# Experts of a routed block: the second product with the activations stationary, five tiles of 128 slots, and the last rows from GpSimd

## The chip, the core and the metric

The kernel runs on one core of one Trainium2 chip. Its time is the device time of one execution in microseconds (us). A core has TensorE (PE, with its weight loads listed apart as PEld), VectorE (DVE), ScalarE (ACT), GpSimd (POOL) and SyncE (SP), which issues most DMAs. Each engine takes its own instructions in order, and they meet through semaphores.

## What is computed

4096 tokens (32 sequences of 128) are embedded, pass one causal attention layer, and then a feed-forward layer with eight experts. Each token goes to one expert, and an expert takes at most 641 tokens. All arithmetic is float32. The part that matters here:

```python
capacity = int(N / E * CAPACITY_FACTOR) + 1          # 4096 / 8 * 1.25 + 1 = 641
eb = buf[:E * capacity].reshape(E, capacity, D)      # D = 256
h = gelu(einsum('ecd,edf->ecf', eb, W1) + b1[:, None, :])   # F = 1024
y = einsum('ecf,efd->ecd', h, W2) + b2[:, None, :]
out = where(valid, y[slot], 0.0) * combine_w[:, None]       # added to the residual
```

## The kernel before

The first part (up to 322 us of the profile) is attention and routing. It writes one row of 260 floats for each routed token to a DRAM table `rows_of_slots`: the residual (256), the routing weight (column D), mean and reciprocal deviation of the layer norm (D+1, D+2) and the token's number (D+3). Each expert has SL = 648 rows there.

The second part, `expert_phase`, does the experts one after the other, all on one core. 641 slots are rounded up to six tiles of 108 (NT = 6, TS = 108, SL = 648), or two halves of 324 columns (NH). float32 products are made of rounded pairs: a value x is kept as a high part (`hh`, `weh`, `xh`, written by ACT as a rounded copy) and a low part (`hl`, `wel`, `xl`, the difference, made by DVE), and each product takes three matmuls, high by high, high by low, low by high. For one expert the engines do this:

- **Up product** (L1260, 16 steps u): the weights are stationary (128 x 128), the tokens move (324 columns). A step is 6 matmuls into one of four PSUM banks S0, S1, C0, C1. ACT makes the gelu `gl` (L1184) and its rounded copy `hh` (L1178), and DVE makes `hl` (L1342). In the last six steps DVE also normalises the next expert's tokens (`xne`, L1304).
- **Down product** (L1277, 4 steps v): W2 is stationary, `hh`/`hl` move (324 columns), 24 matmuls a step, into banks PV and M2 in turn. The result stands with the features on the partitions. ACT adds the bias b2 (`yt`, L1199), PE transposes it back (`back`, L1227, 12 transposes of 128 x 108 into C0 and C1 for an expert, tiles 0 to 2 within the down product and 3 to 5 after steps u = 0 and u = 1 of the next expert), DVE multiplies by the routing weight and adds the residual (`finish`, `ys`, L1329), and POOL scatters the rows of a tile to the output by an indirect DMA (L1138).
- **For the next expert**, within the down product: ACT rounds W1 and W2 in eight pieces of 512 columns (`weh`, L1152), DVE subtracts (`wel<-w_raw,weh`, L1294, both inputs in SBUF, two pieces in each step v), PE transposes the normalised tokens (`turn`, L1215, three times four transposes), ACT and DVE make `xh` and `xl` of them.
- **SP** loads the weights of the expert after next into `w_raw`, then waits for all six scatters of the present expert and loads the next rows (L1104).

The bank of step v is free for step v + 2 when `yt` has been made.

Of the kernel before, what the change touches and what calls it, by code (L numbers as in the profile page):

```python
# [75 lines left out]
def lm_block(nc, x, table, wq, wk, wv, wo, wg, W1, b1, W2, b2, out):  # L76
# [28 lines left out]
    with ExitStack() as whole:  # L105
# [68 lines left out]
def attention_phase(nc, sb_in, sem, v):  # L174
    x, table, wq, wk, wv, wo, wg, b1, b2 = (v[n] for n in ("x", "table", "wq", "wk", "wv", "wo", "wg", "b1", "b2"))
# [15 lines left out]
    with ExitStack() as scope:  # L191
# [25 lines left out]
        bias_raw = sb("bias_raw", [E * (FC + KC), P], F32)  # L217
# [108 lines left out]
        def sync(sp):  # L326
# [4 lines left out]
            sp.dma_start(bias_raw[0:E * FC, :], b1.rearrange("e (c p) -> (e c) p", p=P)).then_inc(d_c, 16)  # L331
            sp.dma_start(bias_raw[E * FC:, :], b2.rearrange("e (c p) -> (e c) p", p=P)).then_inc(d_c, 16)
# [21 lines left out]
            def step(n, i):  # L354
# [270 lines left out]
        def tensor(pe):  # L625
# [30 lines left out]
            pe.wait_ge(d_c, 48)  # L656
            pe.transpose(bC[0][:, 0:E * (FC + KC)], bias_raw[:, :], identf[0:E * (FC + KC), 0:E * (FC + KC)]
# [184 lines left out]
        def vector(dve):  # L842
# [70 lines left out]
            dve.tensor_copy(biases[:, :], bC[0][:, 0:E * (FC + KC)]).then_inc(v_bias, 1)  # L913
# [140 lines left out]
def expert_phase(nc, sb_in, sem, v):  # L1054
    D, E, KC, F, FC, SL, NT, TS, NH, N = (v[n] for n in ("D", "E", "KC", "F", "FC", "SL", "NT", "TS", "NH", "N"))
# [5 lines left out]
    down_bank = [bPV, bM2]  # L1061
    turn_bank = [bM0, bM1]
    back_bank = [bC[0], bC[1]]
    NU = 2 * FC
    DOWN = 2 * KC
    TURNS = NT // 2
    PIECES = 8
    PC = 2 * KC * F // PIECES
    assert KC * F == FC * D and TURNS % 2 == 1

    with ExitStack() as scope:
# [3 lines left out]
        xs = [sb(f"xs{q}", [TS, NT, ROW], F32) for q in range(2)]  # L1075
        xn = sb("xne", [TS, NT, D], F32)
# [10 lines left out]
        d_out = [sem(f"d_out{j}") for j in range(NT)]  # L1087
        e_turn, e_up, e_down, e_back = sem("e_turn"), sem("e_up"), sem("e_down"), sem("e_back")
        a_xh, a_weh, a_gelu, a_hh, a_yt = (sem("a_" + n) for n in ("xh", "weh", "gelu", "hh", "yt"))
        v_exn, v_xl, v_wel, v_hl, v_ys = (sem("v_" + n) for n in ("exn", "xl", "wel", "hl", "ys"))  # L1090
# [10 lines left out]
        def sync(sp):  # L1101

            def load_rows(e):
                sp.dma_start(xs[e.slot][:, :, :], slots[bass.ds(e.times(SL), SL), :].rearrange("(p j) c -> p j c", j=NT)  # L1104
                             ).then_inc(d_xs[e.slot], 16)

# [3 lines left out]
            rows_of = slots[0:SL, :].rearrange("(p j) c -> p j c", j=NT)  # L1110
            for r in range(TURNS):
                sp.dma_start(xs[0][:, 2 * r:2 * r + 2, :], rows_of[:, 2 * r:2 * r + 2, :]).then_inc(d_first[r], 16)
            load_rows(expert(0, 1))

            def step(n, i):
                e, e2 = expert(n, i), expert(n, i + 2)
                if e2:
# [6 lines left out]
                    for j in range(NT):  # L1124
                        hold(sp, d_out[j], e.times(16, 16))
# [3 lines left out]
            for j in range(NT):  # L1129
                sp.wait_ge(d_out[j], 16 * E)  # L1130
# [255 lines left out]
```

## Time and profile before

| | |
|---|---|
| median of 3 runs | 595.01 us (592.73 to 596.51) |
| the profiled execution | 592.0 us, its span 590.3 us |
| granted TensorE clock over the span | 0.969 |
| PE busy | 543.5 us (92%) |
| one expert (from one down product to the next, mean of seven) | 31.05 us |
| from the last expert's down product to the end of the span | 29.3 us |

The profiled execution is 3.0 us below the median of the runs. The profile's page gives busy times of the engines, the chain of work that ended last, and groups of instructions by line. The trace behind it lists single instructions with start and duration.

### The profile page before, as it was taken

Reading aid. Unit: us, or ns where it says so; the run is one execution under the profiler, and the core shown is the slowest. Engines: PE = TensorE matmul, PEld = TensorE weight load, DVE = VectorE, ACT = ScalarE, POOL = GpSimd, SP = SyncE. Lnnn points to the kernel's source line nnn. Section 1 sums busy time; section 2 is a strip of 40 time slices with the busy share of each in tenths; the row PEclk is TensorE's granted clock in tenths of the full one; section 3 lists DMA queues with packets and bytes.
Section 4 is the critical chain, followed back from the end, with each engine's and each line's share of the span. In section 5 each row is a group of like instructions: output and inputs, shape, how many; then the busy total and the mean of one; then the engine's idle time right before and its main releaser. Section 6 shows DMA issues by size and latency. Waiting matters only on the chain.

```text
span 590.3 us, 13904 instructions
## 1 busy us (share of the span) xinstructions
PE 543.5 (92%) x5040; PEld 472.2 (80%) x5045; DVE 398.7 (68%) x1076; ACT 349.2 (59%) x760; POOL 264.8 (45%) x345
## 2 busy tenths in 40 slices
PE   6857899999999999998887999999999999999991
PEld 3646687787788887775553899999999999999990
DVE  7346689999999999988545475656575655665511
ACT  3323666666666666664523676858594949494820
POOL 6745677768667766765534004040403122121212
PEclk9977999999999999998899899999999999999996
DMA  3799986777777777771113601515150606020000
GB/s 111 190 269 274 280 258 215 239 248 235 235 224 218 234 234 229 200 234 61 38 47 108 190 1 39 191 40 191 31 195 22 202 13 197 28 72 8 29 6 27
DMA packets 44611, 86.51 MB, mean 147 GB/s; under 512 B 7614, under 2 KB 33779, under 8 KB 40896
## 3 DMA queue, kind: packets, MB, share of 16 engines
q1 hardware_dynamic: 37632, 72.83, 40.0%
q0 software_dynamic: 6144, 12.67, 6.9%
q8 instruction: 41, 0.67, 0.5%
q10 hardware_dynamic: 768, 0.13, 0.1%
q14 instruction: 26, 0.21, 0.1%
HBM read 52.64 MB, written 31.74 MB: 143 GB/s over the span
## 4 chain that ended last, share of the span: by engine, by line
PE 76%; DVE 8%; POOL 4%; issue 4%; DMA 4%; ACT 1%; SPq 1%; POOLq 0%; ACTq 0%; DVEq 0%
PE M L689 13%; PE M L1277 10%; PE PV L1277 10%; PE S L1260 10%; PE C L1260 10%; PE PV L835 6%; PE S L728 5%; PE C L741 4%; PE M L631 3%; PE M L710 2%; PE C L1227 2%; DVE mx L921 2%; PE M L1215 2%; DMA ks<-k_parts 1%; POOL h L431 1%
## 5 line engine op out<-in xcount | busy, mean ns | idle before, releaser
L1138 POOL DMA_INDIRECT out_dram<-ys,xs x48 | 51.1, 1064 | 212.4 <-DVE ys L1329 202.6
L536 ACT ACTIVATE pt<-C 128x512 f32<-128x512 f32 x128 | 76.4, 597 | 65.9 <-PE C L741 65.3
L483 POOL TENSOR_SCALAR_AFFINE_SELECT pt<-pt 128x512 f32<-128x512 f32 x128 | 81.1, 640 | 46.1 <-ACT pt L536 45.2
L921 DVE TENSOR_REDUCE mx<-S 128x4 f32<-128x512 f32 x128 | 86.7, 681 | 6.6 <-PE S L728 6.3
L1342 DVE TENSOR_TENSOR hl<-gl,hh 128x324 fp32r<-128x324 f32 x128 | 63.3, 495 | 37.7 <-ACT hh L1178 37.2
L728 PE MATMUL S<-ks,qs 128*128 128x128 bf16 x512 | 52.2, 227 | 10.9 <-issue 6.0
L1178 ACT ACTIVATE hh<-gl 128x324 fp32r<-128x324 f32 x128 | 59.2, 469 | 0.0
L728 PEld LDWEIGHTS S<-ks,qs 128*128 128x128 bf16 x512 | 30.2, 100 | 35.7 <-issue 26.0
L835 PE MATMUL PV<-pt,va 128*32 128x128 f32 x1024 | 55.3, 289 | 3.3 <-ACT os L546 1.6
L741 PE MATMUL C<-qs,ks 97*128 97x128 bf16 x512 | 51.5, 224 | 0.6 <-DMA qs<-nm 0.6
L1329 DVE SCALAR_TENSOR_TENSOR ys<-C,xs 108x256 f32<-108x256 f32 x48 | 21.7, 480 | 40.2 <-PE C L1227 40.2
L1294 DVE TENSOR_TENSOR wel<-w_raw,weh 128x512 fp32r<-128x512 f32 x64 | 40.8, 683 | 0.7 <-ACT weh L1152 0.7
L1260 PE MATMUL S<-xh,weh 128*128 128x324 f32 x128 | 41.2, 322 | 0.0
L1277 PE MATMUL M<-hh,weh 128*128 128x324 f32 x128 | 41.1, 321 | 0.0
L1277 PE MATMUL PV<-hh,weh 128*128 128x324 f32 x128 | 40.4, 316 | 0.0
L1260 PE MATMUL C<-xh,weh 128*128 128x324 f32 x128 | 40.3, 315 | 0.0
L1260 PE MATMUL S<-xl,weh 128*128 128x324 f32 x128 | 39.9, 312 | 0.0
L1277 PE MATMUL M<-hh,wel 128*128 128x324 f32 x128 | 39.9, 312 | 0.0
L1184 ACT ACTIVATE gl<-S,biases 128x324 f32<-128x324 f32 x64 | 34.1, 535 | 9.7 <-PE S L1260 9.7
L1277 PE MATMUL M<-hl,weh 128*128 128x324 f32 x128 | 39.9, 311 | 0.0
L1277 PE MATMUL PV<-hl,weh 128*128 128x324 f32 x128 | 39.9, 311 | 0.0
L1277 PE MATMUL PV<-hh,wel 128*128 128x324 f32 x128 | 39.9, 311 | 0.0
(170 smaller groups left out, 1608.8 us busy)
## 6 DMA issues: line engine op xcount, KB each, us to landing
w_raw<-in_L_ffn_W_dram SPq DMA_DIRECT2D x32, 512.0 KB, 7.5
qs<-q_parts SPq DMA_DIRECT2D x48, 256.0 KB, 4.4
ks<-k_parts SPq DMA_DIRECT2D x48, 256.0 KB, 6.0
q_parts<-qp SPq DMA_DIRECT2D x16, 384.0 KB, 2.5
k_parts<-kp SPq DMA_DIRECT2D x16, 384.0 KB
rows_of_slots<-w_raw SPq DMA_DIRECT2D x6, 877.5 KB, 8.2
xs<-rows_of_slots SPq DMA_DIRECT2D x7, 658.1 KB
out_dram<-h SPq DMA_DIRECT2D x16, 256.0 KB, 7.0
```

Source lines behind the costliest of these rows:

```text
L483: pool.affine_select(out=buf[:, :, :], in_=buf[:, :, :], compare_op=ALU.is_ge, fill=0.0, base=0, pattern=[[0, 4], [1, S]], channel_multipl ...
L536: act.activation(pt[u % 4][:, :, :], bC[u % 2][:, :].rearrange("p (j t) -> p j t", j=4), ACT.Exp, scale=SCALE).then_inc(a_exp, 1)
L689: last = pe.matmul(dst, lhs[a](k), rhs[b](k), start=(m == 0), stop=(m == len(pairs) - 1))
L728: last = pe.matmul(dst[:, j * S:(j + 1) * S], qs[g.slot][:, hh, b * S:(b + 1) * S], ks[g.slot][:, hh, b * S:(b + 1) * S], start=True, stop ...
L741: last = pe.matmul(bC[u % 2][:, j * S:(j + 1) * S], ks[g.slot][0:KS_ROWS + 1, hh, b * S:(b + 1) * S], qs[g.slot][0:KS_ROWS + 1, hh, b * S: ...
L835: last = pe.matmul(bPV[32 * j:32 * j + 32, (u % QUADS) * S:(u % QUADS + 1) * S], va[g.slot][:, b, hh, :], pt[u % 4][:, j, :], start=True, ...
L921: dve.tensor_reduce(mx[g.slot][:, 4 * (u % QUADS):4 * (u % QUADS) + 4, u // QUADS], bS[u % 2][:, :].rearrange("p (j t) -> p j t", j=4), AX ...
L1138: pool.indirect_dma_start(out=outf, out_offset=bass.IndirectOffsetOnAxis(ap=xs[e.slot][:, j, D + 3:D + 4].bitcast(U32), axis=0), in_=ys[j] ...
L1178: act.activation(hh[:, f, cols], gl[u % 4][:, :], ACT.Copy).then_inc(a_hh, 1)
L1260: last = pe.matmul(up_bank[u % 4][:, 0:NH], w1[a][:, k, f * P:(f + 1) * P], xt[b][:, k, half * NH:(half + 1) * NH], start=(m == 0), stop=( ...
L1277: last = pe.matmul(down_bank[v % 2][:, 0:NH], w2[a][:, c, d * P:(d + 1) * P], ht[b][:, c, half * NH:(half + 1) * NH], start=(m == 0), stop ...
L1342: dve.tensor_tensor(hl[:, f, cols], gl[u % 4][:, :], hh[:, f, cols].bitcast(F32), ALU.subtract).then_inc(v_hl, 1)
```

## The change

The slots of an expert are now five tiles of 128 (640) and a rest of XR = 2 rows, SL = 642. Columns 0 to 383 are the first half of the up product and 384 to 641 (258) the second. In the down product the activations are stationary (128 slots) and W2 moves (256 columns), so that the result has the slots on the partitions; the bias step of ACT, `yt`, and all `back` transposes are gone. b2 is loaded, broadcast to 128 partitions, and DVE adds weight times b2 to the residual beforehand (`add_bias`). For the rest row GpSimd multiplies W2 (float32, in `w_raw`, in place, 128 x 2048) by the hidden column of slot 640 (`gx`, 128 x 8), adds in three folds to `acc` (128 x 256), and PE sums over the partitions by one matmul with a stationary of ones, which is the fifth of six in the order (0, 1, 2, 3, EXTRA, 4). SP loads the W2 half for the expert after next only when `acc` has been made.

```diff
+    DOWN = (0, 1, 2, 3, EXTRA, 4)
+    HALF = ((0, 3 * P), (3 * P, SL))
 # SP
-                    for load in load_half:
-                        for k in range(KC):
-                            load(sp, e2.times(1), e2.slot, k)
+                    for k in range(KC):
+                        load_half[0](sp, e2.times(1), e2.slot, k)
+                    hold(sp, p_acc, e.times(1, 1))
+                    for k in range(KC):
+                        load_half[1](sp, e2.times(1), e2.slot, k)
 # POOL, ahead of the six scatters of each expert
+                rest = raw[e.slot][:, KC * F:].rearrange("p (c d) -> p c d", c=FC)
+                wait(pool, v_gx, e.times(1, 1))
+                pool.tensor_tensor(rest, rest, gx[:, :].unsqueeze(2).to_broadcast([P, FC, D]), ALU.mult
+                                   ).then_inc(p_prod, 1)
+                wait(pool, p_prod, e.times(1, 1))
+                pool.tensor_tensor(rest[:, 0:4], rest[:, 0:4], rest[:, 4:8], ALU.add).then_inc(p_fold, 1)
+                wait(pool, p_fold, e.times(2, 1))
+                pool.tensor_tensor(rest[:, 0:2], rest[:, 0:2], rest[:, 2:4], ALU.add).then_inc(p_fold, 1)
+                wait(pool, p_fold, e.times(2, 2))
+                pool.tensor_tensor(acc[:, :], rest[:, 0], rest[:, 1], ALU.add).then_inc(p_acc, 1)
 # ACT
-                    act.activation(yt[:, c, half * NH:(half + 1) * NH], down_bank[v % 2][:, 0:NH], ACT.Identity,
-                                   bias=biases[:, bass.ds(e.times(KC, E * FC + c), 1)]).then_inc(a_yt, 1)
 # PE
-                for v in range(DOWN):
-                        last = pe.matmul(down_bank[v % 2][:, 0:NH], w2[a][:, c, d * P:(d + 1) * P],
-                                         ht[b][:, c, half * NH:(half + 1) * NH],
-                    for j in ((), (), (0, 1), (2,))[v]:
-                        back(e, j)
+                for s, j in enumerate(DOWN):
+                    if j == EXTRA:
+                        wait(pe, p_acc, e.times(1, 1))
+                        pe.matmul(bank[0:XR, 0:D], ones[:, :], acc[:, :], start=True, stop=True).then_inc(e_down, 1)
+                    else:
+                        wait(pe, v_ys, e.times(NX, max(j - 1, 0)))
+                        wait(pe, v_hl, e.times(NU, FC * (1 + j // 3)))
+                            last = pe.matmul(bank[:, 0:D], ht[b][:, c, j * P:(j + 1) * P], w2[a][:, c, :],
+                    if e1 and s < TURNS:
+                        turn(e1, s)
 # DVE
+            def add_bias(e, j):
+                dve.scalar_tensor_tensor(out=row[:, 0:D], in0=b2t[e.slot][0:row.shape[0], :], scalar=row[:, D:D + 1],
+                                         in1=row[:, 0:D], op0=ALU.mult, op1=ALU.add).then_inc(v_b2, 1)
+                    if 2 <= u < 2 + NX:
+                        add_bias(e, u - 2)
+                dve.tensor_tensor(gx[:, :], hh[:, :, NT * P].bitcast(F32), hl[:, :, NT * P].bitcast(F32), ALU.add
+                                  ).then_inc(v_gx, 1)
+                for s, j in enumerate(DOWN):
+                        for _ in range((2, 2, 2, 2, 0, 0)[s]):
+                            split(e1, next(pieces))
+                    finish(e, s, j)
```

How the order changes on GpSimd, in the whole of the expert part. Before, it holds only the 48 scatters:

```order
207 L500 TENSOR_TENSOR h<-ve,halfneg 128x2
208 L415 DMA rows_of_slots<-h,pos 5184x260 x5
209 L1138 DMA out_dram<-ys,xs 4096x256 x48
210 L105 UNCONDITIONAL_BRANCH
```

After the change, from the first expert on (`w_raw` is the float32 copy of the weights):

```order
209 L1162 MEMSET ones 128x2
210 L1169 TENSOR_TENSOR w_raw<-w_raw,gx 128x2048
211 L1172 TENSOR_TENSOR w_raw<-w_raw 128x1024
212 L1174 TENSOR_TENSOR w_raw<-w_raw 128x512
213 L1177 TENSOR_TENSOR acc<-w_raw 128x256
214 L1185 DMA out_dram<-ys,xs 4096x256 x4
215 L1185 DMA out_dram<-ys_extra,xe 4096x256
216 L1185 DMA out_dram<-ys,xs 4096x256
217 L1169 TENSOR_TENSOR w_raw<-w_raw,gx 128x2048
```

Four elementwise instructions of 3840 elements in a partition now stand ahead of each expert's six scatters.

On DVE, from the end of one expert's up product through its down product. Before (`wel` are the differences of the next expert's weights, `ys` the finished tiles):

```order
710 L1342 TENSOR_TENSOR hl<-gl,hh 128x324
711 L1304 TENSOR_SCALAR xne<-xs 108x256
712 L1294 TENSOR_TENSOR wel<-w_raw,weh 128x512 x2
713 L1310 TENSOR_TENSOR xl<-M,xh 128x2x216
714 L1294 TENSOR_TENSOR wel<-w_raw,weh 128x512 x2
715 L1310 TENSOR_TENSOR xl<-M,xh 128x2x216
716 L1294 TENSOR_TENSOR wel<-w_raw,weh 128x512 x2
717 L1329 SCALAR_TENSOR_TENSOR ys<-C,xs 108x256 x2
718 L1310 TENSOR_TENSOR xl<-M,xh 128x2x216
719 L1294 TENSOR_TENSOR wel<-w_raw,weh 128x512 x2
720 L1329 SCALAR_TENSOR_TENSOR ys<-C,xs 108x256 x4
```

After:

```order
737 L1380 TENSOR_TENSOR hl<-gl,hh 128x258
738 L1333 TENSOR_SCALAR xne_extra<-xe 2x256
739 L1371 TENSOR_TENSOR gx<-hh,hl 128x8
740 L1323 TENSOR_TENSOR wel<-w_raw,weh 128x512 x2
741 L1365 SCALAR_TENSOR_TENSOR ys<-PV,xs 128x256
742 L1345 TENSOR_TENSOR xl<-M,xh 128x2x256
743 L1323 TENSOR_TENSOR wel<-w_raw,weh 128x512 x2
744 L1365 SCALAR_TENSOR_TENSOR ys<-M,xs 128x256
745 L1345 TENSOR_TENSOR xl<-M,xh 128x2x256
746 L1323 TENSOR_TENSOR wel<-w_raw,weh 128x512 x2
747 L1365 SCALAR_TENSOR_TENSOR ys<-PV,xs 128x256
```

Each `ys` now stands behind a pair of `wel` from the first tile on, and `gx`, for which GpSimd waits, stands just ahead of the first pair.

## Rows read from the trace of the kernel before

**Rows 1.** Page, busy time of engines: us, share of the span, instructions.
```profile
PE 543.5 (92%) x5040; PEld 472.2 (80%) x5045; DVE 398.7 (68%) x1076; ACT 349.2 (59%) x760; POOL 264.8 (45%) x345
```

**Rows 2.** Chain of work in time, one expert: start us, us, what.
```profile
405.73 3.58 PE PV L1277 x24
409.68 3.60 PE M L1277 x24
...
417.24 0.44 PE C L1227 x4
418.05 3.60 PE M L1277 x24
421.86 0.90 PE S L1260 x6
422.76 0.44 PE C L1227 x4
...
436.83 3.57 PE PV L1277 x24
```

**Rows 3.** Windows, seven experts and the last: A:B us, busy of each engine, PEclk, DMA share, GB/s.
```profile
343.65:561.03 217.38, 217.38 (x1515) 216.62 (x1514) 131.90 (x271) 153.52 (x330) 45.12 (x42) 1.00 0.27 85
```

**Rows 4.** Timeline of PE, attention part: matmuls with 256 moving columns.
```profile
201.66 0.28 PE L689 MATMUL M<-xth,wl 128*128 128x256 f32 x1
...
202.72 0.28 PE L689 MATMUL M<-xth,wl 128*128 128x256 f32 x1
```

**Rows 5.** Groups by line and form, POOL: out<-in xcount | busy us, mean ns.
```profile
L483 POOL TENSOR_SCALAR_AFFINE_SELECT pt<-pt 128x512 f32<-128x512 f32 x128 | 81.1, 640 | 46.1 <-ACT pt L536 45.2
...
L493 POOL TENSOR_TENSOR kp<-kr,kp 128x512 bf16<-128x512 f32 x16 | 18.5, 1159 | 7.6 <-ACT kp L558 7.6
...
L425 POOL TENSOR_TENSOR std<-ve,rs 128x2 f32<-128x2 f32 x16 | 3.1, 196 | 1.3
```

**Rows 6.** Timeline, DVE and POOL in three places: start us, us, engine, line, what.
```profile
91.80 1.81 POOL L483 TENSOR_SCALAR_AFFINE_SELECT pt<-pt 128x512 f32<-128x512 f32 x3
...
91.89 0.59 DVE L1039 SCALAR_TENSOR_TENSOR pl<-over,cn 128x16 f32<-128x16 f32 x1
...
92.51 1.13 DVE L1042 TENSOR_TENSOR pm<-pl,oh 128x16 f32<-128x16 f32 x1
...
290.23 1.13 DVE L1039 SCALAR_TENSOR_TENSOR pl<-over,cn 128x16 f32<-128x16 f32 x1
...
291.39 0.17 DVE L1042 TENSOR_TENSOR pm<-pl,oh 128x16 f32<-128x16 f32 x1
...
310.93 0.72 POOL L500 TENSOR_TENSOR h<-ve,halfneg 128x2 f32<-128x2 f32 x1 [6.25 <-DVE ve L880]
310.94 0.20 DVE L1011 TENSOR_TENSOR leq<-lg,lmax 128x16 f32<-128x16 f32 x1
```

**Rows 7.** Timeline, DVE, down product from 405.73 us.
```profile
407.86 0.49 DVE L1342 TENSOR_TENSOR hl<-gl,hh 128x324 fp32r<-128x324 f32 x1
...
408.59 1.28 DVE L1294 TENSOR_TENSOR wel<-w_raw,weh 128x512 fp32r<-128x512 f32 x2
...
421.90 0.48 DVE L1329 SCALAR_TENSOR_TENSOR ys<-C,xs 108x256 f32<-108x256 f32 x1 [1.44 <-PE C L1227]
```

**Rows 8.** Groups in the attention part, a plain float32 product on PE.
```profile
L662 PE MATMUL C<-wgs,meanw 128*128 128x8 f32 x4 | 0.5, 245 | 0.0
```

**Rows 9.** Timeline, the end of the last expert.
```profile
575.57 0.38 PE L1227 MATMUL C<-identf,yt 128*108 128x128 f32 x2
...
578.06 1.00 POOL L1138 DMA_INDIRECT out_dram<-ys,xs  x1 [2.44 <-DVE ys L1329]
...
581.95 0.99 POOL L1138 DMA_INDIRECT out_dram<-ys,xs  x1 [0.30 <-issue]
```

**Rows 10.** Windows around a wait of PE: as in rows 3, PEclk after the busy times.
```profile
322.00:325.00 3.00, 0.27 (x3) 0.22 (x3) 0.93 (x3) 0.00 (x0) 0.00 (x0) 1.00 0.86 243
325.00:328.00 3.00, 2.60 (x11) 1.53 (x11) 2.31 (x6) 1.06 (x2) 0.00 (x0) 0.53 0.92 248
```

More of the change, by code:

```diff
@@ L1074, in expert_phase @@
         hl = sb("hl", [P, FC, SL], F32R)
-        xs = [sb(f"xs{q}", [TS, NT, ROW], F32) for q in range(2)]
-        xn = sb("xne", [TS, NT, D], F32)
+        xs = [sb(f"xs{q}", [P, NT, ROW], F32) for q in range(2)]
+        xe = [sb(f"xe{q}", [XR, ROW], F32) for q in range(2)]
+        b2t = [sb(f"b2t{q}", [P, D], F32) for q in range(2)]
+        xn = sb("xne", [P, NT, D], F32)
+        xne = sb("xne_extra", [XR, D], F32)
+        gx = sb("gx", [P, FC], F32)
+        acc = sb("acc", [P, D], F32)
+        ones = sb("ones", [P, XR], F32)
         xh = [sb(f"xh{q}", [P, KC, SL], F32R) for q in range(2)]
@@ L1080, in expert_phase, with row_of @@
         wl = [sb(f"wel{q}", [P, 2 * KC * F], F32R) for q in range(2)]
-        gl = [sb(f"gl{i}", [P, NH], F32) for i in range(4)]
-        yt = sb("yt", [P, KC, SL], F32)
-        ys = [sb(f"ys{j}", [TS, D], F32) for j in range(NT)]
+        gl = [sb(f"gl{i}", [P, 3 * P], F32) for i in range(4)]
+        ys = [sb(f"ys{j}", [P, D], F32) for j in range(NT)] + [sb("ys_extra", [XR, D], F32)]
         d_xs = [sem(f"d_xs{q}") for q in range(2)]
         d_first = [sem(f"d_first{r}") for r in range(TURNS)]
[L1087 to L1090, printed above, removed]
+        d_out = [sem(f"d_out{j}") for j in range(NX)]
+        e_turn, e_up, e_down = sem("e_turn"), sem("e_up"), sem("e_down")
+        a_xh, a_weh, a_gelu, a_hh = (sem("a_" + n) for n in ("xh", "weh", "gelu", "hh"))
+        v_exn, v_xl, v_wel, v_hl, v_ys, v_b2, v_gx = (
+            sem("v_" + n) for n in ("exn", "xl", "wel", "hl", "ys", "b2", "gx"))
+        p_ones, p_prod, p_fold, p_acc = (sem("p_" + n) for n in ("ones", "prod", "fold", "acc"))
+        def row_of(e, j):
+            return xe[e.slot][:, :] if j == EXTRA else xs[e.slot][:, j, :]
         def expert(n, off):
@@ L1150, in split @@
                 wait(act, d_raw[q], e.round(32 * KC, 32 * KC))
-                wait(act, e_down, e.back(1).times(DOWN))
+                wait(act, e_down, e.back(1).times(NX))
                 act.activation(wh[q][:, c * PC:(c + 1) * PC], raw[q][:, c * PC:(c + 1) * PC], ACT.Copy
@@ L1173, in rounded @@
                     half, f = divmod(u, FC)
-                    cols = slice(half * NH, (half + 1) * NH)
-                    wait(act, e_down, e.back(1).times(DOWN, (half + 1) * KC))
+                    at, to = HALF[half]
+                    wait(act, e_down, e.back(1).times(NX, (half + 1) * 3))
                     wait(act, a_gelu, e.times(NU, u + 1))
-                    act.activation(hh[:, f, cols], gl[u % 4][:, :], ACT.Copy).then_inc(a_hh, 1)
+                    act.activation(hh[:, f, at:to], gl[u % 4][:, 0:to - at], ACT.Copy).then_inc(a_hh, 1)
                 for u in range(NU):
@@ L1190, in step @@
                 pieces = iter(range(PIECES))
-                for v, count in enumerate((3, 2, 2, 1)):
-                    if e1:
+                if e1:
+                    for r, count in enumerate((3, 3, 2)):
                         for _ in range(count):
                             split(e1, next(pieces))
-                    half, c = divmod(v, KC)
-                    wait(act, e_down, e.times(DOWN, v + 1))
-                    hold(act, e_back, e.times(NT))
-                    act.activation(yt[:, c, half * NH:(half + 1) * NH], down_bank[v % 2][:, 0:NH], ACT.Identity,
-                                   bias=biases[:, bass.ds(e.times(KC, E * FC + c), 1)]).then_inc(a_yt, 1)
-                    if e1 and v < TURNS:
-                        turned(e1, v)
+                        turned(e1, r)
             steps(act, step)
@@ L1356, in vector @@
             steps(dve, step)
-            for j in (3, 4, 5):
-                finish(expert(0, E - 1), j)
         return {"sync": sync, "gpsimd": gpsimd, "scalar": scalar, "tensor": tensor, "vector": vector}
```

194 lines of the change are left out of this document (99 added, 95 removed).

## Prediction

> **What bounds the kernel now.** I read the page's busy times first: PE is busy 92% of the span, no other engine over 68% [rows 1]. A share is only an average, so I then read the chain of work in order of time for one expert [rows 2] and the windows over seven experts [rows 3]. The chain is PE alone, and PE is busy for all 217.38 us of seven experts, at the full clock of 1.00. So an expert costs what PE issues for it: 217.38 / 7 = 31.05 us. DVE (131.9 us there) and POOL (45.1 us) have room on the average [rows 3]. Taking work from PE therefore pays at once, as long as nothing that is put on the others makes PE wait.
>
> The 31.05 us are, from [rows 2]: 96 up matmuls and 96 down matmuls of 324 columns, each group of 24 taking 3.58 us and lying next to the following one at 0.148 us a matmul, so 14.2 + 14.2; three turns, 409.68 - 405.73 - 3.58 = 0.37 each, 1.1; and the transposes back, 0.44 for the pair of tiles 0 and 1, as much for 3 and 4, and about half of that for each of the tiles 2 and 5 (418.05 + 3.60 to 421.86 is 0.21), together 1.32.
>
> **The change, part by part.** *Products.* The width that the new ones have is in the trace: nine steps between ten matmuls of 256 columns take 202.72 - 201.66 = 1.06, so 0.118 us each, their weight loads hidden [rows 4]. The slope to 324 columns is (0.148 - 0.118) / 68 = 0.44 ns a column, so 384 columns take 0.1745 and 258 take 0.119. Up: 48 x 0.1745 + 48 x 0.119 = 14.09, against 14.21: -0.12. Down: 120 x 0.118 = 14.16 against 14.21: -0.05. A tile of the down product takes 24 x 0.118 = 2.84.
>
> *Transposes.* The back transposes go: -1.32 an expert, with ACT's `yt`, which was hidden. The turns keep their twelve transposes, now 128 wide instead of 108; I take +0.05 each, +0.15.
>
> *The matmul with ones.* It is plain float32, and the trace has such a product recorded as two instructions for each one in the program, 4 rows for two (L662) [rows 8]. It has only 8 columns there. Bounds: once 0.118 below, four times that, 0.47, above; I take 0.36.
>
> Without any new wait that is -0.12 - 0.05 - 1.32 + 0.15 + 0.36 = -0.98 for each of the first seven experts, -6.9.
>
> *GpSimd's chain.* Its length: a TENSOR_TENSOR of 512 elements takes 1.159, one of 2 elements 0.196 [rows 5]. Per element that is 2.26 ns if all of it is counted, or (1.159 - 0.196) / 510 = 1.9 ns on top of a fixed 0.19 us. The four instructions of 2048, 1024, 512 and 256 elements take 4.6 + 2.3 + 1.2 + 0.6 = 8.7 by the one and 4.1 + 2.1 + 1.2 + 0.7 = 8.1 by the other. The rows are of a subtraction with a bf16 output, nearest to hand. I take 2.2 ns, 8.6 with the fixed part inside, and 0.12 for each of three handovers: 9.0. The Trainium skill's GPSIMD Engine Reference (3.1, Elementwise, side-by-side) gives 4497 ns for a float32 add of 2048; by it the first instruction would be 0.1 shorter than by the row, and the sum would not move.
>
> The chain starts when `gx` is made, behind the last `hl`. Before, the last `hl` starts 2.1 after the down product [rows 7], late because DVE waited for rows of the next expert; with the second half narrower and the rows asked for earlier (below), I put `gx` at 2.0 after the down product's start D. Undisturbed, `acc` would be ready at D + 11.2. PE needs it after four tiles and three turns, 4 x 2.84 + 3 x 0.42 = 12.6. So by lengths alone the chain is just hidden, with 1.4 to spare.
>
> *But the two engines don't run side by side.* DVE's L1042, 16 elements with both inputs in SBUF, takes 0.17 at 291.39 and 1.13 at 92.51 [rows 6]. At 92.51 POOL is inside three affine selects back to back, 0.64 each [rows 5], which end at 91.80 + 1.81 = 93.61; the DVE instruction ends at 93.64. The one ahead of it starts at 91.89, inside the first select, and ends at 92.48, 0.04 behind that one. There are nine such cases, the first and the last in [rows 6]: DVE instructions with two SBUF inputs that start inside an affine select, each ending 0.02 to 0.04 after that select or after the next one. The page SBUF, State Buffer of the Trainium skill (Who interferes with whom) has it as a rule: of a DVE instruction with two SBUF inputs and a GpSimd instruction that reads SBUF, the later one blocks fully until the other has ended. The trace agrees, with 1.13 against 0.17.
>
> `wel<-w_raw,weh` has two SBUF inputs, eight of them an expert, 1.28 for two [rows 7], 0.62 each in a row. (`ys` and `xl` read one input from PSUM; I take it that they pass.) The conversions stand on DVE between the `ys`, for which PE waits two tiles later (banks PV and M2), and they begin with `gx`, just when POOL's chain begins. So I lay them out in series, in two orders:
>
> - DVE's pair runs through: pair 1 from D + 2.05 to 3.3; multiply 3.3 to 7.85; `ys` 0 and `xl` in its shade; pair 2 to 9.1; fold 9.1 to 11.4; pair 3 to 12.6; fold to 13.8; pair 4 to 15.0; last fold to 15.7. PE could have gone on at 12.6 and goes at 15.8: 3.2 lost.
> - The engine that waits goes first: multiply 2.7 to 7.2, the second `wel` after it, `ys` 0 at 8.3 instead of 3.3. Tile 2 waits for it until 8.4 instead of 6.5; the third and fourth `wel` fall around the folds, `ys` 1 comes at 13.0, tile 3 starts at 13.1 instead of 11.7. The chain ends at 13.2, in time. 1.9 + 1.4 = 3.3 lost.
>
> Either way about 3.3 an expert, by 1.9 ns an element 2.7, and with `gx` 1 us later 4.3. Seven experts convert weights for a next one, so 7 x 3.3 = +23.1 (18.9 to 30). The last has no `wel`, and its chain ends at 11.2 as PE's four tiles end at 11.4.
>
> *The end.* From D = 561.03 the span before has 29.3. PE ends the down product at 575.6, the last scatter starts at 581.95 and ends at 582.94, and 7.35 follow [rows 9]. After: the tiles end at D + 11.4 + 0.36 + 2.84 = 14.6, the last `ys` at 15.4. But POOL sends nothing before its chain is through at 11.2, and scatters come every 1.3 [rows 9]: four to 16.4, the extra one to 17.7, the last to 19.0. With 7.35 behind it, 26.3: -3.0.
>
> *What costs nothing.* `add_bias`, six of about 0.48, lies in the up product between `hl` of 0.5 to 0.56 while a step there takes PE 1.05. If a step should be fuller than that, `hl` falls behind, and `gx` with it; that is the 4.3 above. The W2 load for the expert after next waits for `acc`, some 20 us ahead of its use. The scatters queue behind POOL's chain, and the next rows wait for them; the last scatter then ends about 4.5 us into the next up product. Before, three tiles were transposed only 0.9 us into it and later [rows 2] and then scattered at 1.3 each, to about 6 us in, so nothing is later.
>
> **Sum**, against the profiled execution: 592.0 - 6.9 + 23.1 - 3.0 = 605.2. It lies 3.0 below the median, so in the terms of the runs 608.
>
> **The rivals.** *1. The chain is hidden* (faster). The two engines share as their lengths say, because a plain TENSOR_TENSOR leaves room or the conversions slip in. For it: at 310.93 a POOL TENSOR_TENSOR of 0.72 does not hold up a DVE instruction that starts in it, 0.20 [rows 6]; but that one reads 2 elements. Against it: nine of nine cases with long reads. It gives 595 - 9.9 = 585. It decides where the wait of PE is under 9.9 / 7 = 1.4 us an expert, which in the series above needs an element under about 1.6 ns. *2. The wait costs the clock too.* Before the first expert PE waited 2.7 us, and in the window from 325 to 328 the clock was 0.53, that is 1.2 instead of 2.4 GHz for most of it [rows 10]. One wait of 3.2 an expert could bring such a stretch each time; 3 us at 0.53 lose 1.4, seven times 10: 618, and 622 with the upper prices. Against it: in the second order the wait is in two parts. *3. Part of the chain goes for free* (an element at 1.6 ns, or half of the conversions come between the folds): 1.5 an expert, 10.5 - 9.9, so 595 to 597, no change.
>
> **How the numbers follow.** The wait as laid out, with the clock kept, 0.50 (601 to 615, predicted 608); with the clock 0.20 (612 to 622); rival 3 0.10; rival 1 0.20. A change under 1%, 6 us, can't be told from none here. Faster 0.20, same 0.10, slower 0.70. The range from 594 to 622 leaves out rival 1.
>
> **What would show it.** Right: in the down product of the first seven experts, pairs of `wel` that take several us instead of 1.28, each ending 0.03 behind a GpSimd instruction; PE waiting for `acc` or for `ys` 3 us an expert; an expert of 31.05 - 0.98 + 3.3 = 33.4 us; the last one without any such wait. Groups of L1312 at 2.84 for 24, and no C transposes. Wrong: pairs of `wel` at 1.28 beside the multiply, or a multiply under 3.3 us. An expert of 30.1 us would be rival 1; a clock under 1.00 in the experts, rival 2.

## The result, and the profile after

| | before | after |
|---|---|---|
| median of 4 runs each, same chip | 595.76 us (592.73 to 597.15) | 766.97 us (765.13 to 767.90) |
| ratio after / before | | 1.286 (95%: 1.283 to 1.290) |
| span of the profiled execution | 590.3 us | 765.3 us |
| granted TensorE clock over the span | 0.969 | 0.856 |
| start of the first expert's up product | 328.58 us | 498.65 us |
| from there to the end of the span | 261.7 us | 266.7 us |

The kernel became slower by 29%, where 608 us (594 to 622) was predicted. The last two rows say where: 170 of the 175 us were lost before the first expert begins, in a part of which the prediction doesn't speak. The expert part, which it did cost, grew by 5.0 us, not by 13.

The page of the kernel after, its busy times as in [rows 1], then slices of the span (forty of 19.1 us), then the chain by engine and by line:

```profile
PE 564.6 (74%) x5157; PEld 481.2 (63%) x5157; DVE 450.3 (59%) x1132; ACT 323.5 (42%) x728; POOL 341.3 (45%) x378
...
PE   7664170807245150999999988899999999999993
...
PEclk9966575856758575899999998999999999999997
...
PE 37%; DMA 30%; DVE 13%; issue 8%; POOL 4%; ACT 4%; SPq 3%; POOLq 0%; ACTq 0%; DVEq 0%
DMA q_parts<-qp 20%; PE M L687 8%; DVE wel L1323 6%; DMA rows_of_slots<-w_raw 5%; PE S L1293 4%; PE C L1293 4%; PE PV L833 4%; PE S L726 4%; PE M L1312 3%; PE PV L1312 3%; PE C L739 3%; DMA qs<-q_parts 3%; ACT hh L1226 2%; DVE xne L1333 2%; SPq L338 2%
```

PE's row is full from the seventeenth slice on and has holes before it. The chain, PE for 76% of the span before, is now PE for 37% and DMA for 30%, and a fifth of the span is one kind of transfer, `q_parts<-qp`, which the diff doesn't touch.

In the order of time, five of the chain's six steps of over 20 us (start, us, what):

```profile
48.41 35.29 DMA q_parts<-qp
87.97 38.99 DMA q_parts<-qp
...
144.78 25.49 DMA q_parts<-qp
...
231.78 26.94 DMA q_parts<-qp
262.86 37.51 DMA rows_of_slots<-w_raw
```

The one such transfer that stands in the chain of before took 4.66 us. What stands ahead of two of them on SP (timeline: start, us, instruction; the time is that of issuing, and issuing a `q_parts` took 0.36 in the kernel before):

```profile
42.14 0.48 SPq L377 DMA_DIRECT2D rows_of_slots<-w_raw  x1
48.41 8.36 SPq L360 DMA_DIRECT2D q_parts<-qp  x1
...
87.49 0.44 SPq L377 DMA_DIRECT2D rows_of_slots<-w_raw  x1
87.97 13.43 SPq L360 DMA_DIRECT2D q_parts<-qp  x1
101.45 8.58 SPq L363 DMA_DIRECT2D k_parts<-kp  x1
```

Ahead of each stands a `rows_of_slots<-w_raw`, the six transfers that blank the table of slots, one in each step of the attention part. Windows in the middle of such waits (A:B, busy of PE, PEld, DVE, ACT and POOL, clock, DMA share, GB/s), and one of the kernel before during its third blank:

```profile
112.00:116.00 4.00, 0.00 (x0) 0.00 (x0) 0.00 (x0) 0.00 (x0) 0.00 (x0) 0.52 0.07 30
116.00:120.00 4.00, 0.00 (x0) 0.00 (x0) 0.00 (x0) 0.00 (x0) 0.00 (x0) 0.50 0.06 27
```

```profile
75.00:79.00 4.00, 4.00 (x53) 3.33 (x52) 1.94 (x5) 2.31 (x4) 3.69 (x5) 1.00 0.89 346
```

No engine of the core does anything for these stretches, and of 16 DMA engines one works (0.06 is 1/16), at 27 GB/s or little more. A blank is 869.4 KB, that is 890,240 bytes; at 27 GB/s it takes 33 us. Before, 0.89 of the DMA engines were busy at 346 GB/s in such a stretch.

One edit of the change, which the diff ahead of the prediction doesn't print, explains the number (lines between these are left out):

```diff
-    SPREAD = E * SL // 96 // BLANKS
+    BR = E * SL // 48
+    SPREAD = 48 // BLANKS
-        blank = raw[0][0:96, 0:SPREAD * ROW]
+        blank = raw[0][0:BR, 0:SPREAD * ROW]
-                        sp.dma_start(slots[:, :].rearrange("(p a m) c -> p a (m c)", p=96, a=BLANKS)[:, c], blank
+                        sp.dma_start(slots[:, :].rearrange("(p a m) c -> p a (m c)", p=BR, a=BLANKS)[:, c], blank
```

The table had 8 x 648 = 5184 rows and was blanked from 96 partitions, 9 rows each in every one of six transfers. With SL = 642 it has 5136 rows and is blanked from `BR` = 107 partitions, 8 rows each, and 107 is prime. The Trainium skill (DMA: Bandwidth & Descriptors, Why a DMA increments its semaphore by 16 and not by 1) has the rule: a transfer is split over k engines, the largest k up to 16 that divides the slowest dimension on both sides, with 127 partitions, k = 1, as an example. The trace agrees: one sixteenth. The Trainium skill also says (same page, Queues, rings and completion order) that each engine takes its ring in order. By that the share of `q_parts` for that one engine waits behind the blank; the chain shows the wait, 25 to 39 us where it was 4.66.

The sum: from one blank to the next the step took (120.2 - 42.2) / 5 = 15.6 us before and (262.86 - 42.14) / 5 = 44.1 after. That is 28.5 more in each of five steps, 142.7; from the last blank to the first expert it was 208.4 and is 235.8, 27.4 more; together 170. (Some 4 us of them have another cause, see experiment 1.) Their first and last starts are in these rows, after and then before (one line's instructions; the last row of before is its time to landing):

```profile
L377 SPq DMA_DIRECT2D rows_of_slots<-w_raw x6: 433/438/482, 42.1 to 262.9; - x6
```

```profile
L379 SPq DMA_DIRECT2D rows_of_slots<-w_raw x6: 580/580/1201, 42.2 to 120.2; - x6
...
DMA to landing us min/median/max: 7.6/8.2/8.9
```

Now the expert part. Between the first and the last down product, the window that answers to [rows 3]:

```profile
513.89:738.03 224.14, 217.97 (x1613) 211.27 (x1611) 178.89 (x321) 130.99 (x302) 112.62 (x70) 0.99 0.29 91
```

217.38 became 224.14, +6.8 for seven experts (+0.97 each), and PE, which never waited there before, waits 6.2. One down product of it, DVE and then POOL (timelines):

```profile
547.93 0.15 DVE L1371 TENSOR_TENSOR gx<-hh,hl 128x8 f32<-128x8 f32 x1
548.01 1.27 DVE L1323 TENSOR_TENSOR wel<-w_raw,weh 128x512 fp32r<-128x512 f32 x2
549.22 0.47 DVE L1365 SCALAR_TENSOR_TENSOR ys<-PV,xs 128x256 f32<-128x256 f32 x1
549.67 0.69 DVE L1345 TENSOR_TENSOR xl<-M,xh 128x512 fp32r<-128x512 f32 x1
550.28 5.82 DVE L1323 TENSOR_TENSOR wel<-w_raw,weh 128x512 fp32r<-128x512 f32 x2
556.02 0.47 DVE L1365 SCALAR_TENSOR_TENSOR ys<-M,xs 128x256 f32<-128x256 f32 x1
```

```profile
548.18 4.58 POOL L1169 TENSOR_TENSOR w_raw<-w_raw,gx 128x2048 f32<-128x2048 f32 x1 [13.65 <-DVE gx L1371]
552.84 2.71 POOL L1172 TENSOR_TENSOR w_raw<-w_raw 128x1024 f32<-128x1024 f32 x1
555.63 1.61 POOL L1174 TENSOR_TENSOR w_raw<-w_raw 128x512 f32<-128x512 f32 x1
557.32 1.08 POOL L1177 TENSOR_TENSOR acc<-w_raw 128x256 f32<-128x256 f32 x1
```

The first pair of `wel` runs through in 1.27, as in [rows 7]. The second takes 5.82: its two instructions come to their end behind the multiply (552.76) and behind the first fold (555.55), by 0.2 and 0.5, and the `ys` behind them comes at 556.02. PE has to wait for that one:

```profile
556.55 0.39 PE L1312 MATMUL M<-weh,hh 128*128 128x256 f32 x1 [0.78 <-DVE ys L1365]
556.77 0.28 PE L1312 MATMUL M<-weh,hl 128*128 128x256 f32 x1
556.89 0.28 PE L1312 MATMUL M<-wel,hh 128*128 128x256 f32 x1
```

Seven such waits are all that PE has in the expert part behind its start (waits: us, times, longest), 0.78 in six experts and 1.48 in one:

```profile
PE M L1312 <- DVE ys L1365: 6.2, 7, 1.5
```

At the end, from the last down product (738.03) to the end of the span, 27.3 us where it was 29.3.

### The profile page after: what moved, and what is told of

Its sections match the earlier page's. It is cut to its first block, busy times and chain, and to the rows that moved or that the text cites. A ratio compares the mean times of both kernels' runs of the same rounds, so it can differ in the third digit from the quotient of the medians.

```text
span 765.3 us, 14159 instructions
## 1 busy us (share of the span) xinstructions
PE 564.6 (74%) x5157; PEld 481.2 (63%) x5157; DVE 450.3 (59%) x1132; ACT 323.5 (42%) x728; POOL 341.3 (45%) x378
## 4 chain that ended last, share of the span: by engine, by line
PE 37%; DMA 30%; DVE 13%; issue 8%; POOL 4%; ACT 4%; SPq 3%; POOLq 0%; ACTq 0%; DVEq 0%
DMA q_parts<-qp 20%; PE M L687 8%; DVE wel L1323 6%; DMA rows_of_slots<-w_raw 5%; PE S L1293 4%; PE C L1293 4%; PE PV L833 4%; PE S L726 4%; PE M L1312 3%; PE PV L1312 3%; PE C L739 3%; DMA qs<-q_parts 3%; ACT hh L1226 2%; DVE xne L1333 2%; SPq L338 2%
## 5 line engine op out<-in xcount | busy, mean ns | idle before, releaser
L1169 POOL TENSOR_TENSOR w_raw<-w_raw,gx 128x2048 f32<-128x2048 f32 x8 | 35.7, 4461 | 123.8 <-DVE gx L1371 123.8
L1380 DVE TENSOR_TENSOR hl<-gl,hh 128x258 fp32r<-128x258 f32 (+1 forms) x128 | 62.7, 492 | 36.6 <-ACT hh L1226 25.0
L1323 DVE TENSOR_TENSOR wel<-w_raw,weh 128x512 fp32r<-128x512 f32 x64 | 77.1, 1247 | 0.7 <-issue 0.7
L1233 ACT ACTIVATE gl<-S,biases 128x384 f32<-128x384 f32 (+1 forms) x64 | 34.2, 536 | 65.0 <-PE S L1293 61.1
L1226 ACT ACTIVATE hh<-gl 128x258 fp32r<-128x258 f32 (+1 forms) x128 | 60.4, 479 | 0.0
L1312 PE MATMUL PV<-weh,hh 128*128 128x256 f32 x192 | 55.1, 287 | 0.0
L1312 PE MATMUL PV<-weh,hl 128*128 128x256 f32 x192 | 54.0, 281 | 0.0
L1312 PE MATMUL PV<-wel,hh 128*128 128x256 f32 x192 | 53.7, 280 | 0.0
L833 PEld LDWEIGHTS PV<-pt,va 128*32 128x32 f32 x1024 | 21.0, 112 | 47.9 <-POOL pt L481 29.2
L413 POOL DMA_INDIRECT rows_of_slots<-h,pos x32 | 34.1, 1067 | 36.2 <-DMA rows_of_slots<-w_raw 29.7
## 6 DMA issues: line engine op xcount, KB each, us to landing
rows_of_slots<-w_raw SPq DMA_DIRECT2D x6, 869.4 KB
```

The source lines that it names most:

```text
L833: last = pe.matmul(bPV[32 * j:32 * j + 32, (u % QUADS) * S:(u % QUADS + 1) * S], va[g.slot][:, b, hh, :], pt[u % 4][:, j, :], start=True, ...
L1226: act.activation(hh[:, f, at:to], gl[u % 4][:, 0:to - at], ACT.Copy).then_inc(a_hh, 1)
L1312: last = pe.matmul(bank[:, 0:D], ht[b][:, c, j * P:(j + 1) * P], w2[a][:, c, :], start=(m == 0), stop=(m == len(terms) - 1))
L1323: dve.tensor_tensor(wl[q][:, c * PC:(c + 1) * PC], raw[q][:, c * PC:(c + 1) * PC], wh[q][:, c * PC:(c + 1) * PC].bitcast(F32), ALU.subtrac ...
L1380: dve.tensor_tensor(hl[:, f, at:to], gl[u % 4][:, 0:to - at], hh[:, f, at:to].bitcast(F32), ALU.subtract).then_inc(v_hl, 1)
```

## The experiments

**1. The table of before, in the kernel after.** Everything of the change stays but the number of rows in the table, so that it can be blanked from 96 partitions again. And the reverse: the kernel before with its table blanked from 107 partitions, 8 rows each; that covers 5136 of its 5184 rows, and a seventh, small transfer blanks the last 48 (the lines on its semaphore are left out).

```diff
# kernel after, blanks from 96
-    slots = nc.dram_tensor("rows_of_slots", [E * SL, ROW], F32)
+    slots = nc.dram_tensor("rows_of_slots", [5184, ROW], F32)
-    BR = E * SL // 48
-    SPREAD = 48 // BLANKS
+    BR = 96
+    SPREAD = 9
# kernel before, blanks from 107
-    SPREAD = E * SL // 96 // BLANKS
+    SPREAD = 8
+    MAIN = 107 * 48
-        blank = raw[0][0:96, 0:SPREAD * ROW]
+        blank = raw[0][0:107, 0:SPREAD * ROW]
-                        sp.dma_start(slots[:, :].rearrange("(p a m) c -> p a (m c)", p=96, a=BLANKS)[:, c], blank
+                        sp.dma_start(slots[0:MAIN, :].rearrange("(p a m) c -> p a (m c)", p=107, a=BLANKS)[:, c], blank
+                if i == 1:
+                    sp.dma_start(slots[MAIN:E * SL, :], blank[0:48, 0:ROW]).then_inc(d_init, 16)
```

> The changed kernel with one thing put back: the DRAM table of slots has 5184 rows again (the last 48 are never used), and the six DMAs that blank it go out from 96 partitions with 9 rows each instead of 107 partitions with 8 rows. Theory A (the 107-partition source puts each blanking DMA on one DMA engine, and SP's other transfers queue behind it): the attention part is back to that of before, the first up product starts at about 329.5 us instead of 498.65, and the time is about 600 us, 1.005 to 1.015 of before. Rival B (the attention part is slow for another reason, such as the table's row count, the biases or the longer code): it stays above 740 us.

> The kernel before with one thing taken from the change: the first 5136 rows of its table are blanked by six DMAs from 107 partitions with 8 rows each, and the last 48 rows by one small DMA from 48 partitions. Nothing of the experts is touched. Theory A: each blanking DMA lasts 34 us on one engine, as in the changed kernel, and the time is about 755 to 770 us. Rival B: it stays near 596 us.

With 96 the kernel after takes 601.18 us (9 runs, 599.15 to 603.89), 1.008 of before (1.004 to 1.011; before 597.94 on that chip); its first expert starts at 332.97. With 107 the kernel before takes 762.18 us (one run), its clock 0.855. It has none of the new products, biases or chains, and its page's chain shows the same waits (chain in time, two of the six):

```profile
89.42 39.43 DMA q_parts<-qp
...
264.44 37.17 DMA rows_of_slots<-w_raw
```

So the 107 partitions make 27 of the 29%: 1.276 with everything else of the change in place (1.286 / 1.008), 1.275 with nothing else of it (762.18 / 597.94, one run). Without them the rest of the change costs 0.8%.

With 96 the first expert still starts 4.4 us later in the profile than before (332.97 against 328.58), so the blanks are 166 of the 170 us, some 28 for each of the six. Of the 4.4, 0.8 is new waiting behind the last rows of the table, which land 8.3 us ahead of the first expert and not 7.5, because a load of b2 stands there; in the kernel after it is in the chain too:

```profile
491.98 5.27 DMA b2t<-in_L_ffn_b_dram
```

The other 3.6 lie in the attention part. There is only one profile of the kernel before, of an execution 3 us below its median, and the medians are only 3.2 us apart, so how much of the 3.6 is the change stays open.

**2. Is it the number of its divisors?** Two more counts in the kernel after: 108 (the largest divisor up to 16 is 12) and 106 = 2 x 53 (the largest is 2). A rival would have it that more than 96 partitions is what hurts, or the size of a partition's piece. The edit for 108 is shown (the table has 5184 rows); for 106 it is 106, 9 and 5724.

```diff
-    BR = E * SL // 48
-    SPREAD = 48 // BLANKS
+    BR = 108
+    SPREAD = 8
```

> As e1_blank96, but blanked from 108 partitions with 8 rows each, so with the packets of 8320 bytes of the changed kernel and one partition more. Theory A in the form of the Trainium skill (DMA: Bandwidth & Descriptors, how k is chosen: the largest number up to 16 that divides the outermost size of both sides): 108 gives 12 engines with 9 packets each, 9 x 0.32 = 2.9 us, hidden, and the time is about 601 us. Rival E (any number that is not a multiple of 16, or packets of this size, is slow): near 767 us or between.

> As e1_blank96, but with a table of 5724 rows blanked from 106 partitions with 9 rows each (packets of 9360 bytes). 106 = 2 x 53, so by theory A two engines with 53 packets each, 53 x 0.37 = 19.6 us a DMA instead of 34.5 on one. One engine lost 168 us in six DMAs, 28 each, so some 6.5 us of each are hidden; two engines lose 6 x 13 = 79 us: about 680 us. Rival E: near 767 us, as with 107, or near 601 us.

108 partitions, with pieces of 8 rows like those of 107, take 600.36 us, not to be told from 96. 106 partitions, with pieces of 9 rows like those of 96, take 680.46. These are one run each; the 80 us between them are far beyond the 10 over which the runs of one kernel spread here. The same waits stand in the chain of 106, shorter (two of six):

```profile
105.33 23.76 DMA q_parts<-qp
...
191.62 22.58 DMA rows_of_slots<-w_raw
```

Its blanks start from 41.9 to 191.6, so 29.9 us a step, +14.3 to the 15.6 of before, where one engine gave +28.5: half. And in a stretch in which no engine of the core works, two sixteenths of the DMA engines do (window, as above):

```profile
210.00:214.00 4.00, 0.00 (x0) 0.00 (x0) 0.00 (x0) 0.00 (x0) 0.00 (x0) 0.64 0.12 49
```

More than 96 partitions (108) costs nothing, and one less than 107 costs half as much. Neither a threshold nor the size of a piece explains that, the divisor does.

**3. What GpSimd's chain costs.** From here on all kernels have the blanks of 96 and are compared with that one. First the chain is left out: a memset of `acc` stands for its four instructions, so the product of the rest row is missing from the outputs (the waits between the four go too; they are not shown).

```diff
-                pool.tensor_tensor(rest, rest, gx[:, :].unsqueeze(2).to_broadcast([P, FC, D]), ALU.mult
-                pool.tensor_tensor(rest[:, 0:4], rest[:, 0:4], rest[:, 4:8], ALU.add).then_inc(p_fold, 1)
-                pool.tensor_tensor(rest[:, 0:2], rest[:, 0:2], rest[:, 2:4], ALU.add).then_inc(p_fold, 1)
-                pool.tensor_tensor(acc[:, :], rest[:, 0], rest[:, 1], ALU.add).then_inc(p_acc, 1)
+                pool.memset(acc[:, :], 0.0).then_inc(p_acc, 1)
```

> As e1_blank96, but GpSimd's four elementwise instructions of each expert are left out and replaced by one memset of acc to zero, so the product with W2 of the rest rows (slots 640 and 641) is missing; all waits stay. Theory C (the chain holds up DVE's wel, and with it ys of tile 1, for which PE waits 0.78 us at tile 3 of each of seven experts): all pairs of wel take 1.28 us, PE's waits at tile 3 are gone, an expert takes about 30.9 instead of 31.7 us, the last expert's scatters are not queued behind the chain and its end is about 3 us earlier; in all 8 to 10 us under e1_blank96. Rival D (the chain costs PE nothing; the rest of an expert is its own work): within 1 us of e1_blank96 apart from the end.

594.75 us (10 runs), 0.996 of before (0.993 to 0.998), 6.4 less than with the chain. `wel` falls from 1325 to 681 ns (groups of DVE behind 333 us, first with the chain, then without), and PE's waits for `ys` are gone:

```profile
L1323 DVE TENSOR_TENSOR wel<-w_raw,weh 128x512 fp32r<-128x512 f32 x56 | 72.1, 1325 | 0.0
```

```profile
L1315 DVE TENSOR_TENSOR wel<-w_raw,weh 128x512 fp32r<-128x512 f32 x56 | 35.9, 681 | 0.0
```

Windows over the seven experts, with the chain and without:

```profile
348.21:570.12 221.91, 216.44 (x1613) 209.74 (x1611) 177.61 (x321) 129.73 (x302) 112.64 (x70) 1.00 0.30 92
```

```profile
349.18:565.10 215.92, 215.92 (x1613) 209.70 (x1611) 147.70 (x321) 134.32 (x302) 45.23 (x49) 1.00 0.30 94
```

31.70 us an expert with it and 30.85 without: 0.86 for the chain, six of the 6.4 us. I had expected 8 to 10 in all, with 3 at the end; the profile's end is only 0.5 shorter (26.8 instead of 27.3).

**4. Is it the chain's presence, or that it reads SBUF?** The four instructions become four memsets of 128 x 2048, which only write (the multiply's edit is shown, the folds' are alike, and a small one for `acc`; again without the rest row's product).

```diff
-                pool.tensor_tensor(rest, rest, gx[:, :].unsqueeze(2).to_broadcast([P, FC, D]), ALU.mult
+                pool.memset(rest, 0.0).then_inc(p_prod, 1)
```

> As e1_blank96, but GpSimd's chain is replaced by four memsets of 128 x 2048 (into the same w_raw) and one of acc, so the product of the rest rows is missing. GpSimd is then busy some 8 us at the same place but reads nothing from SBUF. Theory C (wel is held up by GpSimd's reads): pairs of wel at 1.28 us, PE's wait at tile 3 gone, 6 us under e1_blank96, like e5_no_chain, if the memsets are done by the time PE needs acc. Rival F (any long GpSimd instruction holds wel up): wel of 2 us and more, and the time of e1_blank96.

596.13 us (10 runs), 0.999 of before (0.996 to 1.003). GpSimd is busy 7.6 us in each down product, and `wel` doesn't notice (groups of POOL and of DVE):

```profile
L1171 POOL MEMSET w_raw<- 128x2048 f32 x8 | 14.5, 1814 | 0.5
```

```profile
L1323 DVE TENSOR_TENSOR wel<-w_raw,weh 128x512 fp32r<-128x512 f32 x56 | 35.9, 680 | 0.0
```

Each of its seven down products takes 16.60 us from the first matmul to the next expert's, as without the chain. So neither GpSimd's being busy nor its writing holds `wel` up. What the chain does beyond that is to read SBUF, as the affine selects of [rows 6] do; that the reading locks is what is left, and no run varies it alone. Beside the kernel without the chain, its profile has a longer first up product (18.1 instead of 15.2, PE waiting 2.3 for `xl`) and 2.0 more at the end; that is off the seven experts, and I didn't follow it up.

**5. Where the conversions stand.** If only the `ys` behind the second pair is late, then with no conversions ahead of it PE shouldn't wait. In each bracket of the edit stand the numbers of `wel` ahead of the six `ys`.

```diff
-                        for _ in range((2, 2, 2, 2, 0, 0)[s]):
+                        for _ in range((2, 0, 3, 3, 0, 0)[s]):
```

> As e1_blank96, but with DVE's conversions of the next expert's weights placed 2, 0, 3, 3 ahead of the six ys instead of 2, 2, 2, 2, so that ys of tile 1 does not stand behind a pair that waits for GpSimd. Nothing is left out. Theory C: ys of tile 1 comes right after its tile, PE's 0.78 us at tile 3 is gone in seven experts, 5 us under e1_blank96, if the later conversions don't hold up ys of tile 2. Rival D: no difference.

598.62 us (10 runs), 1.002 (0.999 to 1.005): about 2.6 less than with the old order, where 5 were expected. `ys` of tile 1 is in time, but three `wel` now stand ahead of the next one, and part of the wait moves there (PE's waits):

```profile
PE PV L1312 <- DVE ys L1365: 1.3, 5, 0.3
```

**6. A version from what was learned.** The whole computation: blanks of 96; conversions 2, 0, 1, 5, so that once the chain runs at most one `wel` stands ahead of a `ys` for which PE waits; the two small transposes of the rest row behind those of tile 4 and no longer between them, since the third turn took 0.76 and the other two 0.36 each; and the first load of b2 ahead of the routing's waits on SP, because the first expert had waited for it.

```diff
+            load_bias(expert(0, 0), d_first[TURNS - 1])
-                    if r == TURNS - 1:
+                if r == TURNS - 1:
+                    for k in range(KC):
+                        at = k * (to - first) + P
-                        for _ in range((2, 2, 2, 2, 0, 0)[s]):
+                        for _ in range((2, 0, 1, 5, 0, 0)[s]):
```

> The full computation, from e1_blank96: conversions of DVE placed 2, 0, 1, 5, 0, 0 ahead of the six ys; the first expert's b2 loaded ahead of the waits for routing instead of behind the rows; the two small transposes of the rest rows behind the two of tile 4 instead of between them. Theory C: down product 16.6 us or less instead of 17.45 in seven experts (-6), 0.9 at the first expert's start, 0.1 to 0.2 an expert by the transposes (-1): about 593 us, 0.99 to 0.995 of before. Rival G (as in e6_order, the wait only moves to tile 4, since the later conversions and the folds take turns there): about 597 us.

591.60 us (12 runs, 588.33 to 595.35), 0.991 of before (0.988 to 0.995; before 597.29 there). The window over its seven experts:

```profile
347.55:563.31 215.76, 214.47 (x1612) 209.10 (x1611) 162.39 (x321) 133.65 (x302) 115.44 (x70) 1.00 0.30 94
```

30.82 an expert, with the whole chain in it, where the kernel without the chain has 30.85. They are not alike in the rest: six of the seven down products take 16.37 to 16.47 here and 16.60 there, and the 0.2 lies in the third turn with its moved transposes, 0.52 here and 0.76 there. The seventh takes 17.70; there DVE had waited 1.36 for the rows and b2 to load, and `gx` came 3.6 behind the down product's start. All that PE waits for is `acc`, once, in the second expert:

```profile
L1311 PE MATMUL C<-acc,ones 128*2 128x256 f32 x16 | 4.7, 378 | 1.3 <-POOL acc L1181 1.3
```

It is the first complete version of this change that beats the kernel before, by 0.9%. The three edits were made at once, so their shares weren't measured.

## Why the prediction was wrong

**The step that failed: an edit of the change that had no term.** The sum went over the products, transposes, bias, chain and end, all in the expert part, and ahead of the first expert it took nothing to move. The list "What costs nothing" doesn't name the blanks either. The table's size follows from SL, the blanks' partitions from the table's size, and 8 x 642 / 48 is 107. That was to be read from the whole diff, with no trace needed for it: 96 partitions before, 107 after, and what 107 divides by. Its price could have been bounded from the page of before: 877.5 KB landed in 8.2 us over all engines, so a single one would need many times that. Of the 170 us ahead of the first expert the blanks are 166, some 28 for each of the six (experiments 1 and 2). I had read no view of the attention part for it, since the change seemed to leave that part alone.

The direction, slower, came out right for another reason than the one given. Without the 107 partitions the change would have been slower by 0.8% (0.4 to 1.1), a case to which I gave 0.10, and not by 2%. The 29% say nothing for the rest of my reasoning: all that `wel` and the chain cost each other (6 us, below) is not a tenth of them.

**The lock**, as I call it that `wel` and GpSimd's chain hold each other up. As foretold, they run one after the other, and a `ys`, with one input in PSUM, passes through a multiply (549.22, 0.47). A chain of memsets doesn't hold `wel` up (experiment 4). Foretold were 3.3 us of wait an expert, and it is 0.78 and 0.07 of a slower start, 0.85. The term was mis-sized for three reasons:

- The multiply was put at 4.6 by the rate of a small bf16 subtraction [rows 5]. Its row says 4.58 here, but in the last expert, where no conversions run, 3.60 (1.76 ns an element). About 1.0 of the 4.58 was waiting for the first pair, which I had already counted in series. So the multiply ends at D + 7.2 (D is 545.57), where I had 7.85, although `gx` came at D + 2.4 and not 2.0.
- Of my two orders, what runs begins as the first does, with the whole pair, and goes on as the second, by single instructions: multiply, one `wel`, fold, one `wel`, fold. With one conversion or none ahead of each fold, `acc` is ready at 558.40, D + 12.8, and not 15.7 as in the first order (13.2 in the second).
- So the chain was through ahead of PE's need: its matmul with ones comes at D + 14.0. Of the `ys` only one was late, by 0.78. The sign in the trace that I had named (each `wel` ending 0.03 behind a GpSimd instruction) held only roughly, with 0.2 and 0.5.

The sizes come nearest to rival 3 (part of the conversions between the folds, 1.5 us an expert). By the line that I drew for rival 1, a wait under 1.4, the kernel should even have become faster; it didn't, because the products saved 0.2 and not 0.98. Two slips in my sums: 3840 elements at 2.2 ns are 8.4 us and not 8.6, and rival 2 with the upper prices is 608 + 7 + 10 = 625 and not 622. The first is worth about 1 us in seven experts, and the second doesn't enter the forecast.

POOL in the last expert (timeline) shows the lengths alone: from 740.11 to 748.37 the chain takes 8.3 us with its handovers, where I took 9.0.

```profile
740.11 3.60 POOL L1169 TENSOR_TENSOR w_raw<-w_raw,gx 128x2048 f32<-128x2048 f32 x1 [13.16 <-DVE gx L1371]
743.79 2.40 POOL L1172 TENSOR_TENSOR w_raw<-w_raw 128x1024 f32<-128x1024 f32 x1
746.26 1.29 POOL L1174 TENSOR_TENSOR w_raw<-w_raw 128x512 f32<-128x512 f32 x1
747.63 0.74 POOL L1177 TENSOR_TENSOR acc<-w_raw 128x256 f32<-128x256 f32 x1
...
754.87 0.99 POOL L1185 DMA_INDIRECT out_dram<-ys,xs  x1 [0.30 <-issue]
```

**The products.** Foretold -0.98 an expert; without the chain it is 30.85 against 31.05, -0.2. I multiplied instructions by the pace inside a run, and left out what a change from one kind of matmul to another costs: behind a turn or behind the matmul with ones, the first matmul of a tile is followed by the next one after 0.20 to 0.23 instead of 0.12 (556.55, 556.77, 556.89). Tiles take 2.82 to 3.02 and not 2.84, five of them +0.44; an up product of four groups +0.16; the third turn, with the rest row's small transposes in it, 0.76 and not 0.42 (all three turns +0.2); the matmul with ones 0.52 and not 0.36. That sums to 0.97, of which 0.2 is what my terms for before had fallen short of its 31.05.

**The end.** Foretold -3.0, measured -2.0. The last scatter ends at 755.86, 17.8 behind the down product, earlier than the 19.0 foretold, mostly because the chain is through earlier. But 9.4 to 9.5 us follow it, not 7.35, in every kernel with this change, the one without the chain too; in the kernel before with 107 partitions it is 7.3. So it comes with the change to the expert part; what these 2.1 us are I don't know.

**The clock (rival 2).** It fell in one expert of seven, behind the wait of 1.48, which ended at 620.65 (windows):

```profile
620.00:623.00 3.00, 2.35 (x11) 2.35 (x12) 3.00 (x6) 0.00 (x0) 2.76 (x3) 0.63 0.00 0
623.00:626.00 3.00, 3.00 (x19) 2.43 (x19) 2.61 (x7) 0.00 (x0) 2.39 (x3) 0.81 0.78 215
```

That expert's down product took 19.67, the other six 17.45; 0.7 of the 2.2 is wait, 1.5 clock. Its `gx` came at D + 3.05 and not 2.4, for a reason that I didn't follow up. After waits of 0.78 it didn't fall, and in the profile with the blanks of 96, where no such wait is over 0.8, it stays at 1.00. In the attention part it did a great deal: it stood at 0.50 at the end of the long waits for the blanks (116 to 120), and PE's work behind them began at that level (0.50 from 128 to 136, 0.52 from 180 to 184, then 1.00), which is part of the price of a blank; how much wasn't measured.

**Altogether for the expert part:** foretold +13.2. Measured with the blanks of 96: waits 7 x 0.85 = 6.0, products 7 x -0.2 = -1.5 (215.92 - 217.38), the end -2.0, the first up product 0.2, so +2.7. The kernel after has the 2.2 of the one clocked-down expert on top.

## What to carry to other kernels

When a change alters a size, follow the size to every place that is derived from it, above all to the partition count (the slowest dimension) of each transfer, and look at its largest divisor up to 16: here 107 partitions put the whole transfer on one DMA engine and 106 on two, and what was queued behind it waited. In a forecast, a GpSimd instruction that reads SBUF should be laid out against DVE instructions with two SBUF inputs one by one, and the instruction of DVE that others wait for should stand ahead of those, not behind them. For a sum of many short groups of matmuls, take the time from group to group in the trace and not the pace within one.

## What the runs showed of the hardware that was not expected

- One DMA engine moves rows of 8320 bytes at 27 GB/s; a transfer of 869.4 KB from 107 partitions takes 33 us by that, where 96 partitions with 877.5 KB landed in 8.2 us, in the midst of other traffic.
- Six such transfers, each small beside the whole, cost 166 us, since SP's later transfers share the engine: the price is paid in the queue (`q_parts` 25 to 39 us instead of 4.66) and not by anyone who waits for the blanks, except once at the end (37.51).
- DVE and GpSimd alternate by single instructions when each has several in a row that hold up the other's, and an instruction's recorded time holds its wait: the multiply is recorded at 4.58 for 3.60 of work, a `wel` at 2.7 to 2.9 for 0.68.
- GpSimd's memset of 128 x 2048 float32 takes 1.81 us, half of the multiply, and DVE runs beside it at full pace.
